# Causal attention on one core: sub-blocks of 128 queries in the column tiles of the product with V, and one closing product

## The reference

```python
Q = embeddings @ W_Q; K = embeddings @ W_K; V = embeddings @ W_V
scores = einsum('bqd,bkd->bqk', Q, K) / sqrt(32)
masked = where(causal, scores, -inf)
probs = softmax(masked, axis=-1)
out = einsum('bqk,bkd->bqd', probs, V)        # t = t + out
```

## Time and profile before

| | us |
|---|---|
| median of 3 runs (lowest, highest) | 4871.97 (4871.01, 4875.54) |
| span of the profiled execution, first to last instruction | 4868.0 |
| attention L2, L3 (within the span, about) | 1558 to 3057, 3201 to 4705 |
| TensorE busy over the span | 4346.1 (89%) |
| VectorE, ScalarE, GpSimd busy over the span | 3127.4, 2852.8, 1430.0 |
| product with V (L487), busy, L2 and L3 | 354.3 and 356.8 |

### The profile page before, as it was taken

How to read it: one execution, slowest core, us unless ns; L and a number is a source line. 1 busy time by engine, 2 the same in 40 slices (tenths; PEclk the granted TensorE clock), 3 DMA queues, 4 the chain that set the end, 5 groups by cost and what they waited for, 6 DMA issues and landing times. The chain is left out here.

```text
span 4868.0 us, 100989 instructions
## 1 busy us (share of the span) xinstructions
PE 4346.1 (89%) x39002; PEld 2617.2 (54%) x39002; DVE 3127.4 (64%) x6052; ACT 2852.8 (59%) x5802; POOL 1430.0 (29%) x2222
## 2 busy tenths in 40 slices
PE   4888888886985999999999999779999999999985
PEld 2666666664332555555555555545555555555544
DVE  4777777777886556666666665446666666666653
ACT  2777777774883555555565565325556555555541
POOL 4323322330001233334333331123333333334220
PEclk9999999998986899999999999779999999999987
DMA  1200000000000000000000000000000000000003
GB/s 24 32 2 2 2 3 2 3 2 4 1 1 0 2 2 2 2 2 2 2 2 2 2 2 2 5 1 2 2 2 2 2 2 2 2 2 2 2 6 54
DMA packets 348175, 22.49 MB, mean 5 GB/s; under 512 B 346388, under 2 KB 347700, under 8 KB 347700
## 3 DMA queue, kind: packets, MB, share of 16 engines
q1 hardware_dynamic: 347700, 16.03, 4.5%
HBM read 7.88 MB, written 6.42 MB: 3 GB/s over the span
## 5 line engine op out<-in xcount | busy, mean ns | idle before, releaser
L551 DVE TENSOR_REDUCE L3a_mx<-L3a_r 128x1 f32<-128x512 f32 (+4 forms) x1344 | 771.1, 628 | 330.0 <-PE L3a_r L415 322.5
L551 DVE TENSOR_REDUCE L2a_mx<-L2a_r 128x1 f32<-128x512 f32 (+4 forms) x1344 | 771.0, 628 | 330.0 <-PE L2a_r L415 322.5
L415 PE MATMUL L2a_r<-L2a_vT,L2a_qT 32*128 32x512 f32 (+3 forms) x3488 | 880.6, 526 | 13.0 <-DVE L2a_mx L551 12.3
L415 PE MATMUL L3a_r<-L3a_vT,L3a_qT 32*128 32x512 f32 (+3 forms) x3488 | 880.6, 526 | 13.0 <-DVE L3a_mx L551 12.3
L514 ACT ACTIVATE L3a_e<-L3a_r 128x512 f32<-128x512 f32 (+3 forms) x1344 | 669.0, 570 | 268.0 <-PE L3a_r L394 264.4
L514 ACT ACTIVATE L2a_e<-L2a_r 128x512 f32<-128x512 f32 (+3 forms) x1344 | 669.1, 570 | 265.5 <-PE L2a_r L394 261.9
L394 PE MATMUL L3a_r<-L3a_qT,L3a_vT 32*128 32x512 f32 (+4 forms) x3488 | 770.1, 510 | 5.0 <-DMA L3a_qT<-L3a_nm 4.8
L394 PE MATMUL L2a_r<-L2a_qT,L2a_vT 32*128 32x512 f32 (+4 forms) x3488 | 769.8, 511 | 3.7 <-DMA L2a_qT<-L2a_nm 3.6
L1434 POOL TENSOR_SCALAR win_xw<-win_xr,win_mv,win_rs 32x343 f32<-32x343 f32 (+7 forms) x432 | 327.9, 779 | 702.8 <-ACT win_rs L1222 702.7
L415 PEld LDWEIGHTS L3a_r<-L3a_vT,L3a_qT 32*128 32x128 f32 x3488 | 384.8, 189 | 156.7 <-DVE L3a_mx L551 89.9
L415 PEld LDWEIGHTS L2a_r<-L2a_vT,L2a_qT 32*128 32x128 f32 x3488 | 384.7, 189 | 156.6 <-DVE L2a_mx L551 89.9
(11 more groups left out here) (362 smaller groups left out, 6990.4 us busy)
## 6 DMA issues: line engine op xcount, KB each, us to landing
L2a_qT<-L2a_nm SPq DMA_DIRECT2D x768, 0.5 KB, 2.0
L3a_qT<-L3a_nm SPq DMA_DIRECT2D x768, 0.5 KB, 2.0
T<-in_x SPq DMA_DIRECT2D x16, 384.0 KB, 3.8
out<-T SPq DMA_DIRECT2D x16, 384.0 KB, 4.0
win_mq<-win_nmt SPq DMA_DIRECT2D x256, 3.1 KB, 1.7
win_msk<-in_L_conv_pos_emb SPq DMA_DIRECT2D x49, 0.2 KB
L2a_qT<-L2a_nm SPq DMA_DIRECT2D x32, 0.2 KB, 1.8
L3a_qT<-L3a_nm SPq DMA_DIRECT2D x32, 0.2 KB, 1.8
```

The lines of the kernel that those rows point to most:

```text
L415: return nc.tensor.matmul(bank_of(x)[:, o:o + c1 - c0], QT_[g0:g0 + C, img % 2, q0:q0 + P], VT[g0:g0 + C, img % 2, c0:c1], start=start, st ...
L551: return nc.vector.tensor_reduce(to, frm, AX.X, ALU.max)
```

## The change

In blocks 0 to 5 column tile i now holds the queries 128 i to 128 i + 127 of the block, over all keys, as block 0 did before. Each key tile is multiplied once for each column tile that needs it, 128 queries at a time. `ACC` is then only 128 columns wide, the copy to `O` is 128 columns, and one closing product replaces the four: `O` (128 x 128) is the weight and a block diagonal matrix `WFB` (128 x 132) the moving operand. The tail keeps its form. `O0`, its four copies and its memset go; `WFB` is cleared and filled in the block ahead of the layer's loop.

```diff
-        O = sb("o", [P, 2, QB])
-        O0 = sb("o0", [P, QB])
+        O = sb("o", [P, 2, P])
-        WF = sb("wf", [P, C + 1])
+        WF, WFB = sb("wf", [P, C + 1]), sb("wfb", [P, QT, C + 1])
...
                 nc.vector.memset(MX[:], -3.0e38)
+                nc.vector.memset(WFB[:], 0.0).then_inc(w_zero, 1)
...
-                for g in range(4):
-                    nc.vector.tensor_copy(WF[g * C:(g + 1) * C, C:C + 1], k.ident[0:C, 0:1]).then_inc(w_out, 1)
-                dve.wait_ge(w_out, 8)
-                nc.vector.memset(O0[:], 0.0)
+                dve.wait_ge(w_zero, 1)
+                for g in range(QT):
+                    r = slice(g * C, (g + 1) * C)
+                    nc.vector.tensor_copy(WF[r, C:C + 1], k.ident[0:C, 0:1]).then_inc(w_out, 1)
+                    nc.vector.tensor_copy(WFB[r, g, 0:C], ACC[r, 0:C]).then_inc(w_out, 1)
+                    nc.vector.tensor_copy(WFB[r, g, C:C + 1], k.ident[0:C, 0:1]).then_inc(w_out, 1)
+                dve.wait_ge(w_out, 4 + 3 * QT)
...
-                        for i in range(q_tiles(j)):
-                            r = rows(QT * j + i)
-                            o = i * (C + 1)
-                            out = O[:, FINAL[x] % 2] if j else O0
-                            last = nc.tensor.matmul(bank_of(x)[0:r, o:o + C + 1], out[:, i * P:i * P + r], WF[:],
-                                                    start=True, stop=True)
-                        last.then_inc(item_full, 1)
+                        if j < TAIL:
+                            nc.tensor.matmul(bank_of(x)[:, 0:QT * (C + 1)], O[:, FINAL[x] % 2],
+                                             WFB[:].rearrange("p q c -> p (q c)"),
+                                             start=True, stop=True).then_inc(item_full, 1)
+                        else:
+                            nc.tensor.matmul(bank_of(x)[0:LAST, 0:C + 1], O[:, FINAL[x] % 2, 0:LAST], WF[:],
+                                             start=True, stop=True).then_inc(item_full, 1)
...
-                                same = [y for y in order if y % 4 == u % 4]
-                                cuts = [(C * (u % 4), c0, c1, u == same[0], u == same[-1])]
-                                if j == 0:
-                                    cuts = [(C * i, i * P, (i + 1) * P, u == 0, u == i) for i in range(u, QT)]
-                                for cg, a, b, start, stop in cuts:
-                                    last = nc.tensor.matmul(ACC[cg:cg + C, a:b], V[0:r, img % 2, u, :],
-                                                            E[0:r, n % RE, o + a - c0:o + b - c0],
-                                                            start=start, stop=stop)
+                                if j < TAIL:
+                                    cuts = [(i, i * P - c0, (i + 1) * P - c0, [y for y, c in order if c <= i * P])
+                                            for i in range(c0 // P, QT)]
+                                else:
+                                    cuts = [(u % 4, 0, LAST, [y for y, c in order if y % 4 == u % 4])]
+                                for i, a, b, same in cuts:
+                                    last = nc.tensor.matmul(ACC[C * i:C * i + C, 0:b - a], V[0:r, img % 2, u, :],
+                                                            E[0:r, n % RE, o + a:o + b],
+                                                            start=u == same[0], stop=u == same[-1])
...
-                        if j:
-                            last = nc.scalar.copy(O[:, FINAL[final] % 2, 0:w], ACC[:, 0:w])
-                        else:
-                            for i in range(QT):
-                                g, c = slice(i * C, i * C + C), slice(i * P, i * P + P)
-                                last = nc.scalar.copy(O0[g, c], ACC[g, c])
-                        last.then_inc(acc_read, 1)
+                        nc.scalar.copy(O[:, FINAL[final] % 2, 0:w], ACC[:, 0:w]).then_inc(acc_read, 1)
```

More of the change, by code:

```diff
@@ L223, in bank_of @@
             return R[PLACE[("mask", x[1]) if x[0] == "max" and x[1] in MASK_AT else x] % RING]
-        w_in, w_mm, w_out = sem("w_in"), sem("w_mm"), sem("w_out")
+        w_in, w_mm, w_zero, w_out = sem("w_in"), sem("w_mm"), sem("w_zero"), sem("w_out")
         with nc.Block() as block:
@@ L476, in _ @@
                             pe.wait_ge(acc_read, FINAL[("final", img, j)])
-                        order = [u for bank in score_banks(j) for u, *_ in bank]
+                        order = [(u, c0) for bank in score_banks(j) for u, c0, *_ in bank]
                         for n in range(n0, n1):
@@ L517, in _ @@
                         final = ("final", img, j)
-                        w = width(j)
+                        w = min(width(j), P)
                         act.wait_ge(pv_done, score_at(img, j + 1))
```

## The result

The changed kernel takes 4807.96 us (median of 4 runs, 4801.14 to 4812.99), the kernel before, run beside it, 4873.76 (4871.01 to 4879.46). The ratio is 0.9859, 95% interval 0.9845 to 0.9874: 66 us faster. The forecast was 4767 in a range of 4730 to 4812. So the sign and the range held, but the gain is 66 us and not 105.

What follows compares the result with a forecast made beforehand. TensorE was taken as the bound, an image being a chain on it. Terms of -0.43 - 3.9 + 1.0 = -3.3 us an image, x 32, and +1.3 for setup gave -105 us: 4767 us, range 4730 to 4812.

Steps and rivals of the forecast that it cites:

- Product with V: Batches of blocks 1 to 5: rounds of 128 queries at 0.11 us, gain from empty column tiles, -0.43 us an image.
- D: Rival, batches of blocks 1 to 5: a round does not stay at 0.11 us; at 0.14, 4921 us; chance 0.05.
- Closing products: Six blocks an image, on TensorE: two passes take 0.25 us for 0.91, a gain of 3.9 us an image.
- ScalarE's copies: Copies ahead of the closing products: near 0.2 us for 128 columns where 128x512 takes 0.59; costed at nothing.
- The block ahead of the loop: Setup of each layer: eight more small copies, one memset and its wait gone; net +0.7 us a layer, +1.3 in all.
- The shift wait: TensorE waiting for the shift DMAs before block 5's scores: charged 1.0 us an image, bounds 0 and 1.04.
- The clock: TensorE's granted clock in attention: mean of 0.99 before, allowing some 8 lower stretches a layer; C put 16 more, +27 us.
- A: The forecast itself, the sum of the terms: 4767 us, own range 4752 to 4782; chance 0.58.
- C: Rival: TensorE's standstill in each image makes the granted clock fall more often, 4794 us, with a second DMA wait 4810; chance 0.20.
- B: Rival, before block 5's scores: the shift wait does not bind, 32 us more gain, 4735 us; chance 0.14.

## Why the prediction was right or wrong

**Product with V: right.** The batches came out at 1.88, 2.76 and 2.32 us, the forecast's numbers, a round at 0.11, and the gain is the empty column tiles, as the run with batches of 12 and 8 shows. A batch of 12 without a diagonal, 96 records or 48 products in a row, takes 2324.26 - 2321.50 = 2.76 us too, the pace of block 0's 20 records, so D, the slower rival, has nothing for it. (The prediction's 96 products are these 96 records, and its nine batches are ten with the tail's; no term uses either count.) The Trainium skill, "TensorEngine Tiling (Array Packing)", Performance Considerations (Instruction Overhead), gives about 60 cycles for each matmul; as a cost in series that would have shown here: at the prediction's estimate of 25 ns each, 0.9 us for the 36 more records of a batch of 8. The trace disagrees, since that batch takes 0.04 us more.

**Closing products: mis-sized.** The term was 0.25 us; it measured 0.33, so a gain of 0.58 and not 0.66, 3.5 us an image for 3.9, 13 us over all. The step that failed is the price of the first pass, 0.14, which I took from transposes that follow other products with a 128-column weight. Behind the product with V the records show more: the second pass's weight load starts 0.11 us behind the first's, in both forms, but its product starts another 0.11 us behind that with 132 moving columns and 0.03 with 33. So the first pass takes 0.22 us, where in the old form it took 0.13.

**ScalarE's copies: right.** They fell to 0.27 us, and ScalarE idles 0.59 us behind the one that the earlier trace rows shows at 0.77; behind block 0's copy it idles 1.02 us where it idled 0.23:

```profile
2266.65 0.27 ACT L528 COPY L2a_o<-L2a_acc 128x128 f32<-128x128 f32 x1 [2.40 <-PE L2a_acc L492]
2267.51 0.59 ACT L534 COPY L2a_vT<-L2a_r 128x512 f32<-128x512 f32 x1 [0.59 <-PE L2a_r L448]
```

**The block ahead of the loop: right enough.** From the copy of `WF` to the last write it takes 1.76 us in L2, before 1.43: +0.3 for +0.7. GpSimd, for whose work the loop's first product waits, starts 2.66 us behind that copy of `WF`, before 1.72: +0.9.

**The shift wait: right in place and kind, too small.** It was to take 1.0 us an image, 32 us; it grew by 51.2 - 8.4 = 43 us, 1.3 an image. The run with LEAD 32 shows it was this wait: with the DMAs earlier it is gone. The missing third lies in the DMA chain, which I took at the length it had before; from the end of the reduction to the last landing it takes 7.11 us in the mean of the 32 images, before 6.74. The eight issues took 4.98 us in the earlier trace rows, 5.64 in the row above and 5.13 where TensorE waited 1.08. In the changed kernel's trace 128 of the 1600 issues last over 0.8 us, 79 before, and beside each of these a 16 KB fetch of instructions is under way or begins. Block 5's chain holds such an issue in 24 images of 32, in 9 before. Those 24 are the images in which TensorE waits 1.5 us or more; in the other 8 it waits 0.9 to 1.1 us, as forecast. The change has a third more instructions to fetch (409 packets where the page of before has 313), and the batch that runs beside this chain has 68 records and as many weight loads where it had 20. That every long issue has a fetch beside it is shown, but 116 issues with a fetch beside them are not long; that the one lengthens the other was not tried by itself.

**The clock: the step that failed.** Forecast A left the granted clock as it was and gave the stall its own length only. C said that the stall would lower the clock, 16 more stretches at 1.7 us each; the trace has 16 more falls at 1.6, and the run that fills the wait shows that mechanism. C had 0.20 and A 0.58, because in the earlier trace rows a stall of 0.62 us was alone. Among the shift waits the length tells much: of the 24 of 1.5 us or more 18 had a fall, of the 8 of 0.9 to 1.1 us 2. But length is not all, since the border waits of 0.82 us had one in 13 of 30 before, and what else decides was not tried. So the two steps seem to hang together: by these counts few of the falls would have come with a wait of 1.0 us, though no run tried that. A's own range, 4752 to 4782, is missed; the time lies in the stated range because that was drawn to take in C. That C's 4810 is so near to 4808 is luck in part: its second DMA wait did not come, and its 4794, with the 13 and 11 us that A's terms for the closing products and the wait had wrong, makes 4818.

**The sum again.** Product with V -14, closing products -111, wait +43, falls +26, the block ahead of the loop +1: -55. The two profiled spans differ by 57, the medians by 66. Wait and falls go back to one chain of DMAs, whose code the change did not touch.

**A and B.** B would have needed the wait not to bind; it bound in all 32 images. With LEAD 32 the change is worth 132 us, close to what A's sum gives without its charge for the wait: (0.43 + 3.9) x 32 - 1.3 = 137. With the closing products at their measured 3.5 us an image the sum is 124; the images themselves got 4.10 us shorter, and 0.2 us of that is in no term.

The version that beats both kernels is the changed one with LEAD at 32: 4718.68 us.

## What to carry to other kernels

When work on the bounding engine shrinks, look for a chain that starts on another engine before that work and is waited for behind it: its length does not shrink, and what lay beside it is lost. Move that chain earlier in the same change, by a lead or a queue, and time the change both ways; here the same edit was worth 66 us or 132. And before splitting an operation to fill idle column tiles, see whether cutting its batches at a multiple of four does the same.

## What was not expected of the hardware

A stall of TensorE cost more than its length: filling it with 128 useless products made the kernel 38 us faster. The first pass of a closing product, behind the product with V, shows its own weight load and its stream, 0.22 us (0.33 less 0.11) where one with 33 columns shows 0.13. And every DMA issue of the attention that lasts over 0.8 us (128 of 1600; the median is 0.60) has a fetch of instructions beside it.
